# Two partial tables in place of four for the accumulating scatters of a graph network's averaging layers

## What is computed

```
row, col = (edge_index[0], edge_index[1])
msgs = x[col] * edge_weight[:, None]
agg = jax.ops.segment_sum(msgs, row, num_segments=n)
deg = jax.ops.segment_sum(edge_weight, row, num_segments=n)
deg = jnp.clip(deg, 1.0)[:, None]
h = jnp.concatenate([x, agg / deg], axis=-1)
return h @ W.T + b
```

## Time and profile before

| | us |
|---|---|
| median of 3 runs | 9624.05 (9620.07 to 9639.33) |
| the profiled execution, its time | 9626.48 |
| the profiled execution, its span | 9624.7 |
| GpSimd busy | 6643.4 (69% of the span) |
| TensorE busy (matrix products) | 5439.4 (57%) |
| VectorE busy | 2780.9 (29%) |
| ScalarE busy | 1285.5 (13%) |

### The profile page before, as it was taken

How to read it: one execution, slowest core, us unless ns; L and a number is a source line. 1 busy time by engine, 2 the same in 40 slices (tenths; PEclk the granted TensorE clock), 3 DMA queues, 4 the chain that set the end, 5 groups by cost and what they waited for, 6 DMA issues and landing times.

```text
span 9624.7 us, 115552 instructions
## 1 busy us (share of the span) xinstructions
PE 5439.4 (57%) x27756; PEld 4985.6 (52%) x27757; DVE 2780.9 (29%) x13253; ACT 1285.5 (13%) x3064; POOL 6643.4 (69%) x5897
## 2 busy tenths in 40 slices
PE   4554455544545545776666544455554556677665
PEld 3444444444444445666666444444444546666664
DVE  2222222222222223333333322222222224333333
ACT  1111111111101111111111211111011111111112
POOL 5666656666666665888888666665666667888887
PEclk7677777777777676555555777777677776555556
DMA  3222221111111112555555411111111114555556
GB/s 93 68 69 68 69 56 45 48 46 46 47 44 47 47 46 55 76 75 76 75 75 75 104 44 47 46 46 48 44 45 47 46 46 76 75 75 75 76 75 112
DMA packets 578867, 594.93 MB, mean 62 GB/s; under 512 B 128465, under 2 KB 470718, under 8 KB 578494
## 3 DMA queue, kind: packets, MB, share of 16 engines
q0 software_dynamic: 373312, 383.17, 24.1%
q1 hardware_dynamic: 170246, 190.65, 6.8%
q10 hardware_dynamic: 35192, 19.90, 0.7%
HBM read 431.39 MB, written 161.82 MB: 62 GB/s over the span
## 4 chain that ended last, share of the span: by engine, by line
another core or an unknown queue 33%; issue 21%; DMA 15%; POOL 13%; PE 10%; ACT 3%; DVE 2%; ACTq 1%; DVEq 1%; POOLq 0%; SPq 0%
DMA share<-scat,place 14%; POOL share L478 13%; PE msg L781 6%; ACT sums L587 3%; PE sum L774 2%; DVE acc L979 1%; PE lin L726 1%; ACTq L125 0%; DVEq L972 0%; DVE onehot L967 0%; DVEq L979 0%; ACTq L123 0%; DVE stats L1117 0%; ACTq L122 0%
## 5 line engine op out<-in xcount | busy, mean ns | idle before, releaser
L509 POOL DMA_INDIRECT rows_in<-h_table,edges_i x3328 | 3173.0, 953 | 1855.9 <-issue 1010.1
L478 POOL DMA_INDIRECT share<-scat,place x1664 | 2601.8, 1564 | 581.2 <-issue 334.5
L781 PE MATMUL msg<-sums,mix_w 128*128 128x128 f32 x4992 | 1123.0, 416 | 1833.4 <-ACT sums L587 1176.0
L781 PEld LDWEIGHTS msg<-sums,mix_w 128*128 128x128 f32 x4992 | 1041.3, 318 | 1893.7 <-issue 1609.6
L979 DVE TENSOR_TENSOR acc<-msg,acc 128x16 f32 x4160 | 729.5, 175 | 4329.3 <-issue 1617.4
L806 PE MATMUL msg<-rows_in,sums 16*128 16x128 f32 x3328 | 1273.0, 484 | 894.9 <-ACT sums L601 892.5
L781 PE MATMUL msg<-sums,rel_w 128*128 128x128 f32 x3328 | 755.3, 419 | 1220.4 <-ACT sums L587 849.6
L806 PEld LDWEIGHTS msg<-rows_in,sums 16*128 16x128 f32 x3328 | 884.8, 323 | 983.5 <-issue 501.1
L781 PEld LDWEIGHTS msg<-sums,rel_w 128*128 128x128 f32 x3328 | 701.0, 320 | 1258.0 <-issue 1119.4
L587 ACT ACTIVATE sums<-sum 128x512 f32<-128x512 f32 x1040 | 603.3, 596 | 5157.3 <-remote 3339.1
L774 PE MATMUL sum<-onehot,rows_in 128*128 128x128 f32 x8320 | 1261.6, 315 | 45.8 <-issue 18.9
(11 more groups left out here) (141 smaller groups left out, 2187.1 us busy)
## 6 DMA issues: line engine op xcount, KB each, us to landing
edges_i<-in_src_dram SPq DMA_DIRECT2D x210, 512.0 KB
rows_in<-h_table,edges_i POOLq DMA_INDIRECT x3328
share<-zeros SPq DMA_DIRECT2D x104, 258.0 KB
rows_in<-h_table SPq DMA_DIRECT2D x1664, 8.0 KB
share<-scat,place POOLq DMA_INDIRECT x1664
hT<-share SPq DMA_DIRECT2D x80, 258.0 KB, 4.7
h_table<-rows ACTq DMA_DIRECT2D x65, 256.0 KB
rows_in<-in_x_dram,edges_i POOLq DMA_INDIRECT x832
```

The lines of the kernel that those rows point to most:

```text
L478: nc.gpsimd.indirect_dma_start(out=shares[m][a], out_offset=bass.IndirectOffsetOnAxis(ap=place[:, q // 2, 4 * (q % 2) + a:4 * (q % 2) + a ...
L509: nc.gpsimd.indirect_dma_start(out=rows_in[:, s, :], out_offset=None, in_=rows_of[:, :], in_offset=bass.IndirectOffsetOnAxis(ap=srcT_i[:, ...
L781: last = nc.tensor.matmul(MSG[h][:, 0:HALF * WIN], W[:, n, :], sums[:, h, n, :, :].rearrange("p t v -> p (t v)"), start=(n == 0), stop=(n ...
```

## The change

`SHARES` becomes 2. There are two partial tables in each averaging layer in place of four; tile t of a quad goes to table t mod 2, so an addition now waits for the landing of the one two tiles before. GpSimd no longer adds pairs of tables, and DVE adds the two loaded shares itself, waiting for the loads. SP clears half as many tables and loads half as many shares, and all four buffers for loaded shares now lie in `hT`.

```diff
-SHARES = 4
+SHARES = 2
...
-                                for a in range(SHARES):
-                                    if a == 0:
+                                for t in range(4):
+                                    a = t % SHARES
+                                    if t == 0:
                                         pool.wait_ge(scat_ready[q], k + 2)
-                                    pool.wait_ge(scattered[a], i * 64 + (opened + 16 * q))
-                                    if a < SHARES - 1:
+                                    pool.wait_ge(scattered[a], i * (16 * RING // SHARES) + (opened + 16 * ((4 * q + t) // SHARES)))
+                                    if t < 3:
                                         apart(pool)
                                     else:
                                         pool.sem_inc(quads_left, 1)
                                     nc.gpsimd.indirect_dma_start(
                                         out=shares[m][a], out_offset=bass.IndirectOffsetOnAxis(
-                                            ap=place[:, q // 2, 4 * (q % 2) + a:4 * (q % 2) + a + 1], axis=0),
-                                        in_=scat[:, 4 * q + a, :], in_offset=None, compute_op=ALU.add,
+                                            ap=place[:, q // 2, 4 * (q % 2) + t:4 * (q % 2) + t + 1], axis=0),
+                                        in_=scat[:, 4 * q + t, :], in_offset=None, compute_op=ALU.add,
                                     ).then_inc(scattered[a], 16)
...
-                    def pair_shares(c, j, n):
-                        pool.wait_ge(shares_landed[j], n * 64 + 64 * (shares_before(m, j) + 1))
-                        for a in (0, 2):
-                            ins = nc.gpsimd.tensor_tensor(shares_in[j][:, a, :, :], shares_in[j][:, a, :, :],
-                                                          shares_in[j][:, a + 1, :, :], ALU.add)
-                        ins.then_inc(shares_paired, 1)
-                    chunk_loop(pool, pair_shares)
...
-                    dve.wait_ge(shares_paired, c + (m * CHUNKS + 1))
+                    dve.wait_ge(shares_landed[j], n_in * (16 * SHARES) + 16 * SHARES * (shares_before(m, j) + 1))
+                    apart(dve)
                     both = shares_in[j][:, 0, :, :]
-                    nc.vector.tensor_tensor(both, both, shares_in[j][:, 2, :, :], ALU.add).then_inc(deg_step, 1)
+                    nc.vector.tensor_tensor(both, both, shares_in[j][:, 1, :, :], ALU.add).then_inc(deg_step, 1)
```

More of the change, by code:

```diff
@@ L235, in build @@
         scat = sb("scat", [D, RING, COLS])
-        shares_in = [hT[:, n * RING * COLS:(n + 1) * RING * COLS].rearrange("p (a k c) -> p a k c", a=SHARES, c=COLS)
-                     for n in range(3)] + [scat[:, :, :].rearrange("p (a k) c -> p a k c", a=SHARES)]
+        shares_in = [hT[:, n * SHARES * SUB * COLS:(n + 1) * SHARES * SUB * COLS]
+                     .rearrange("p (a k c) -> p a k c", a=SHARES, c=COLS) for n in range(4)]
         deg = sb("deg", [D, 2, SUB])
@@ L299, in build @@
             sem("round_ends_found"), sem("chunk_rounds_found"), sem("round_ends_in"), sem("round_ends_set"))
-        shares_paired = sem("shares_paired")
         scaled, agg_turned = sem("scaled"), sem("agg_turned")
@@ L378, in _ @@
                     if n % 2 == 0:
-                        sp.wait_ge(summed[3], i * 4 + (n // 2 + 2))
+                        sp.wait_ge(summed[3], i * SHARES + (n // 2 + 2))
                         apart(sp)
@@ L1071, in _, with means @@
                 n_norm = NORM_BEFORE[l]
-                def means(c, j, between):
+                def means(c, j, n_in, between):
                     b = j % 2
                     at = c * 3 + m * 3 * CHUNKS
-                    dve.wait_ge(shares_paired, c + (m * CHUNKS + 1))
+                    dve.wait_ge(shares_landed[j], n_in * (16 * SHARES) + 16 * SHARES * (shares_before(m, j) + 1))
+                    apart(dve)
                     both = shares_in[j][:, 0, :, :]
-                    nc.vector.tensor_tensor(both, both, shares_in[j][:, 2, :, :], ALU.add).then_inc(deg_step, 1)
+                    nc.vector.tensor_tensor(both, both, shares_in[j][:, 1, :, :], ALU.add).then_inc(deg_step, 1)
                     for n in range(3):
@@ L1167, in mean_step @@
                     if is_chunk(c + 3):
-                        means(c + 3, (j + 3) % 4, between)
+                        means(c + 3, (j + 3) % 4, n + (j + 3) // 4, between)
                     else:
```

## The result

The changed kernel takes 10206.49 us (median of 4 runs, 10199.95 to 10216.67). Beside it the kernel before took 9623.9 (4 runs, 9620.07 to 9639.33). The ratio is 1.0603 with a 95% interval from 1.0585 to 1.0621: 583 us slower. Forecast were 10336 us, with a range from 9990 to 10430.

A forecast was written before the change was run, and what follows sets the result against it. The prediction took GpSimd's scatter issue to bound the edge parts, with no landing waited for. From 9626.5 us, +732 (edge parts), -20 (second parts) and 0 (clearing) gave 10338.5, adjusted to 10336 us; range 9990 to 10430.

The forecast's parts named there:

- the likeliest case: Whole kernel: exposed landing and hand-over plus a disturbed landing per half slow the edge parts; 10336 us, chance 63%.
- the step of 4.22: Edge parts: two scatters take landing 3.38, plus 0.04, plus hand-over 0.80 us; a half round takes 16.88 for 14.96.
- The hand-over is exposed: Edge parts: forecast 0.80 us from semaphore to scatter start; the rival hid it at 0.30, giving 9937 us, chance 9%.
- The longer landing of the other rival: Edge parts: landing takes 3.66 us, a step 4.50 and a half 19.6, giving 10569 us; chance 6%.
- Gaps of over 1.5 us: Edge parts, expected sign: one or two such idle gaps before scatters in every eight.
- the clearing at nothing: First relational layer: 56 fewer writes of zeros are hidden behind the gathers, so they save 0 us.
- the held-up landing: Edge parts: SP's 512 KB source-number load delays a scatter's landing, 1.6 us per half, bounds 0 and 2.03.
- The edge term: Both averaging layers' edge parts: 208 halves, each 3.52 us longer, add 732 us.
- nothing absorbs it: Edge parts: the late landing lengthens its table's chain by the full 1.6 us per half; the other table's follows.
- one disturbed landing in each half: Edge parts: the load hits one scatter in eight, the same as today, whose landing is up to 2.03 us late.
- the load falls between two scatters: Edge parts, rival: a small shift lets the scatter's packets through before the load; 10003 us, chance 16%.
- the second parts, -20: Second parts of two layers: earlier first sum by 4.2 us and 12 x 0.5 us in chunks; -20 us, bounds -8 and -32.

The follow-up runs named there:

- the depth-two kernel with four tables: Kernel before, four tables kept, but each scatter waits for the landing of the scatter two before: 9262.44 us, ratio 1.0735.
- the wait-of-one kernel: Kernel before, four tables kept, but each scatter waits for the landing of the one directly before: 12633.26 us, ratio 1.4617.
- the pair with and without it: Changed kernel reusing the first 16 tiles' source numbers every round: 512 KB load still made, 9219.32 us; load cut to 8 KB, 8975.59 us.
- the changed kernel once more: The changed kernel, unaltered, run again on another chip beside the kernel before: 9216.17 us, ratio 1.0664.
- The runs with two and four loads: Kernel before, second parts with DVE adding only tables 0 and 1; loading two tables: 8583.85 us; loading all four: 8619.06 us.

## Why the prediction was right, and where its sizes were off

**Right: the direction, and the likeliest case.** 10206 lies inside the range and inside the likeliest case's own (10150 to 10430). GpSimd waits for landings in the edge parts and nothing else changes its time; the depth-two kernel with four tables shows it.

**Right: the step of 4.22.** Without the load it is 4.20, as a mean over two stages: a landing of 3.35 and a hand-over of 0.79 at the median, and 0.05 for the scatters whose hand-over takes 1.5 us and more. The hand-over is exposed: had it been hidden, the wait-of-one kernel would not have had steps of 4.1. The longer landing of the other rival was not seen; the two undisturbed rows above have 3.42 and 3.49. The mean idle time ahead of a scatter is 17.92 / 8 - 1.55 = 0.69 us (0.76 forecast). Gaps of over 1.5 us are fewer than forecast, 67 in 831 and not one or two in eight.

A longer landing was also what the Trainium skill gave, page "DMA: Bandwidth & Descriptors", section "Anatomy of one DMA": an estimate from its fixed cost and rate put the landing at 3.70 us and a half at 19.76. The runs do not agree (landings of 3.4 us where no load is near, and 17.92 us for a half).

**Right: the clearing at nothing.** The gathers kept their number while the zeros were halved.

**Mis-sized: the held-up landing, 1.6 us in a half; it costs 1.11.** The edge term was 732 us and measured 617. Of the 115 between them 208 x (1.6 - 1.11) = 102 are this, and 208 x (16.88 - 16.81) = 15 the step. That the load does it was right, shown by the pair with and without it. The step that failed is "nothing absorbs it", and "one disturbed landing in each half" with it. That shows in the landings of the changed kernel once more (the trace of its first profile lacks many of the events). In its two layers 275 of 1659 took more than 3.9 us, and without the load 2 of 1657. That is 1.3 in a half, each 1.1 us late (the median of all is 3.4), together 1.48 us in a half. So the lateness was close to the 1.6 that was taken, by luck, since one landing of 1.6 was forecast and more and smaller ones came. But of the 1.48 the kernel pays 1.11.

Where the late ones are, by the same landings: 138 scatters started 1.25 to 1.75 us before a load and landed after 4.0 at the median, 29 started 0.75 to 1.25 before and landed after 5.2, and 96 started 0.25 to 0.75 behind it and landed after 4.2. The 11 that started some 2 us before it landed after 3.6. Of 206 loads none missed: 129 had one landing of over 3.9 us near them, 73 had two, and the mildest case was still 0.47 us late. The rival "the load falls between two scatters" is excluded by that. The kernel before shows the two as well: its scatter of 4508.73, which the forecast read, landed after 5.30, and the next one (4510.59), which it did not read, after 3.82.

How a part is absorbed I only argue from the rows. Two chains with a step of 4.22 leave 4.22 - 2 x 1.86 = 0.50 us between the second of a pair and the next first, and a hold-up that falls on the second of a pair loses 0.5 of itself there. The scatter of 4474.10, the second of a pair, was held up by 1.38; the one that waits for it started at 4479.70, and the next, in the other chain, at 4481.56 and not at 4476.59 + 4.22 = 4480.81, only 0.75 late. Two that are held up by one load also overlap in part, since each delays a chain of its own. No run separates the two effects.

**Mis-sized: the second parts, -20; they gave -41.** Two pieces. DVE's first sum was forecast 5.5 us behind the first load and came 3.96 behind: the forecast kept the landing of 4.7 of a queue with twice the loads, and it became 4.0. And of the 1 us that GpSimd's additions cost a chunk I took half, since PE and ACT have work of their own; over the layer 18.6 us came back, some 6 at the start and the other 12 or so in the chunks, so it was the whole. The runs with two and four loads share it out, roughly: about 25 of 44 us to GpSimd's additions gone, 19 to the fewer loads.

**Open:** why a load that spreads one short row over 128 partitions holds up a scatter's landing by about 1 us at 512 KB and at 64 KB alike. The 8 KB load to 16 partitions did not. Whether it is the number of small pieces, the repeated reading of one address or the order in the queues was not tried. Open too is what makes every 59th and every 112th scatter start late.

## What to carry to other kernels

When accumulating transfers wait for each other, count the time from a transfer's start to its landing and add the hand-over behind the semaphore (here 3.4 + 0.8 us). Divide by the step at which the engine can issue (1.86): the next whole number is the least depth, three here, and one more absorbs landings that other traffic holds up. Fewer partial tables save work in a short stage and take the depth from a long one, so weigh 60 us of a second part against 1550 us of an edge part; and if a short stage's work sits on a slow engine, move the work, not the depth. Don't expect a gain from cutting a disturbing load into pieces: here each piece, spread out, disturbed much as the whole did.

## What the runs showed of the hardware that was not expected

- Eight broadcast loads of 64 KB cost more than one of 512 KB: a half took 18.90 us (1963.6 x 8 / 831) for 17.92. Of its landings 384 in 823 were late, for 140 in 830.
- The hand-over from a landing to the waiting scatter's start is 0.79 us, but in the two-table kernels 1.5 us at every 59th scatter of a layer and 2.2 at every 112th, with the load or without.
- The chips of these runs differ in one kind of work: gathers went at 754 in 950 us on one and 638 on another (1.18 times), while the accumulating scatters took 1.55 us on both and the edge parts differed by 4 us at most (1872.1 and 1849.8 for 1868.3 and 1854.0).
